# Router stage of an attention and mixture-of-experts kernel: older batches' work moved ahead of the new batch's in each step

## The reference, cut to what matters

```python
x = x + _layernorm(_L0_attn_ref(_layernorm(x), ...))          # x: 16 batches x 1024 tokens x 256
x = x + _layernorm(_L0_ffn_ref(_layernorm(x), ...))
# end of _L0_attn_ref:  attn = attn * rms * subln_g * (1 - LAMBDA_INIT);  return attn @ Wo
# start of _L0_ffn_ref, x here is the normalised one:
logits = jnp.einsum('bsd,ed->bse', x, gate_w) + gate_b        # 32 experts
probs = softmax(logits, axis=-2)                              # over the tokens
vals, idx = top 8 tokens of each expert and batch
merged = einsum('bked,bke->bed', x[idx], vals)                # weighted sum of the chosen tokens
# then two small expert layers on merged, and a scatter-add back to the tokens
```

## Time and profile before

| what | value |
|---|---|
| median of 3 runs | 5975.78 us (5975.41 to 5980.85) |
| the profiled execution | 5969.97 us, its span 5968.1 us |
| route, first projection to last copy | 5382.58 to 5699.74 us of the span |
| busy over the whole span | PE 94%, DVE 92%, ACT 83%, POOL 35% |

### The profile page before, as it was taken

The page is one execution under the profiler, slowest core; times in us unless marked ns, Lnnn a source line. Parts: engine busy times, 40 slices in busy tenths (PEclk is TensorE's granted clock), DMA queues, the critical chain, the costliest instruction groups (busy, mean ns, idle before and its releaser), DMA issues. The chain is left out here.

```text
span 5968.1 us, 167678 instructions
## 1 busy us (share of the span) xinstructions
PE 5593.6 (94%) x50896; PEld 1978.1 (33%) x50896; DVE 5489.2 (92%) x6110; ACT 4965.0 (83%) x9174; POOL 2070.4 (35%) x3560
## 2 busy tenths in 40 slices
PE   8878999999999999999999999999999999987776
PEld 4542333333333333333333333333333333325524
DVE  7868999999999999999999999999999999966716
ACT  6665999999999999999999999999999999983313
POOL 7981222222222222222222222222222222235506
PEclk9997999999999999999999999999999999998878
DMA  5671222232222222222232222222222222206587
GB/s 181 204 209 46 52 53 53 53 52 53 52 53 52 53 51 51 52 51 51 50 52 53 53 53 53 52 53 51 53 53 53 53 50 52 50 15 202 198 341 309
DMA packets 408166, 495.27 MB, mean 83 GB/s; under 512 B 132051, under 2 KB 265331, under 8 KB 395235
## 3 DMA queue, kind: packets, MB, share of 16 engines
q1 hardware_dynamic: 406499, 485.74, 32.5%
q10 hardware_dynamic: 1024, 0.53, 0.0%
HBM read 360.60 MB, written 123.21 MB: 81 GB/s over the span
## 5 line engine op out<-in xcount | busy, mean ns | idle before, releaser
L741 DVE TENSOR_REDUCE at_largest<-at_ps_m 128x1 f32<-128x1024 f32 x4096 | 4695.6, 1210 | 43.2 <-PE at_ps_m L845 28.7
L707 ACT ACTIVATE at_e<-at_ps_e 128x512 f32<-128x512 f32 x8192 | 4409.6, 598 | 351.8 <-PE at_ps_e L814 153.3
L831 PE MATMUL at_ps_o<-at_e,at_v 128*32 128x256 f32 (+1 forms) x30720 | 2680.3, 421 | 31.3 <-ACT at_e L707 20.6
L845 PE MATMUL at_ps_m<-k_stack,q_stack 48*128 48x512 bf16 x8192 | 2484.3, 384 | 87.8 <-DVE at_largest L741 55.6
L814 PE MATMUL at_ps_e<-q_stack,k_stack 51*128 51x512 bf16 x8192 | 2514.6, 382 | 8.4 <-issue 2.1
L831 PEld LDWEIGHTS at_ps_o<-at_e,at_v 128*32 128x32 f32 x30720 | 844.9, 149 | 1556.5 <-issue 818.0
L814 PEld LDWEIGHTS at_ps_e<-q_stack,k_stack 51*128 51x128 bf16 x8192 | 567.7, 93 | 1665.4 <-ACT at_e L707 1632.5
L626 POOL TENSOR_TENSOR at_negated<-at_zeros,at_largest_t 128x32 f32<-128x32 f32 x256 | 64.9, 254 | 2165.3 <-DVE at_largest_t L748 2165.3
L845 PEld LDWEIGHTS at_ps_m<-k_stack,q_stack 48*128 48x128 bf16 x8192 | 573.8, 93 | 219.8 <-DVE at_largest L741 188.2
L669 POOL TENSOR_TENSOR at_rms<-at_mean_eps,at_minus_half 128x16 f32<-128x16 f32 x128 | 372.8, 2912 | 10.0
L645 POOL TENSOR_TENSOR at_crossed<-at_totals 128x32 f32<-128x32 f32 x128 | 32.4, 253 | 750.8 <-DMA at_totals<-at_sums 750.8
(11 more groups left out here) (130 smaller groups left out, 3005.6 us busy)
## 6 DMA issues: line engine op xcount, KB each, us to landing
k_stack<-k_parts SPq DMA_DIRECT2D x1536, 64.0 KB
q_stack<-q_parts SPq DMA_DIRECT2D x256, 192.0 KB
q_stack<-q_parts SPq DMA_DIRECT2D x256, 128.0 KB
w_first<-in_w SPq DMA_DIRECT2D x32, 1024.0 KB, 23.4
ex_w_second<-in_w SPq DMA_DIRECT2D x32, 1024.0 KB, 26.1
q_parts<-pr_parts SPq DMA_DIRECT2D x96, 256.0 KB, 2.5
k_parts<-pr_parts SPq DMA_DIRECT2D x96, 256.0 KB, 2.8
pr_x_in<-in_x SPq DMA_DIRECT2D x16, 1024.0 KB, 5.7
```

Source lines behind the costliest of these rows:

```text
L707: nc.scalar.activation(e[:, j % E_BUFS], ps_e[:, bank(u, j)], ACT.Exp, scale=SCALE).then_inc(exp_done, 1)
L741: nc.vector.reduce_max(largest[:, u % 2, j // SIDE, j % SIDE:j % SIDE + 1], ps_m[:, j % 2], AX.X).then_inc(max_done, 1)
L831: last = nc.tensor.matmul(ps_o[32 * tile:32 * tile + 32, columns], v[:, u, tile // 2, first:first + 2 * VD * TILES - kt:TILES], e[:, (QUAD ...
L845: last = nc.tensor.matmul(ps_m[:, j % 2, half * HALF:(half + 1) * HALF], q_stack[rows, u, pair, c, t * P:(t + 1) * P], k_stack[rows, u, pa ...
```

## The change

In each step three engines take the older batches' work first. PE does two banks of transposes, the projection's first half, the other two banks, the projection's second half; then in odd steps the logits, and only after them the transposes of `picked`, which used to come before. ACT does its four copies before `norm_y(0)`, and the exponentials after `norm_y(0)` instead of last. DVE does both gate parts at the step's start. All instructions are the same ones in the same number; waits go with them.

```diff
 # ACT
-                    if y:
-                        act.wait_ge(x1_stored[u % 2], 16 * (2 * i + u // 2) + 16)
-                        norm_y(0)
                     if turn:
...
                             nc.scalar.copy(xn_t[:, u % 2, j % KC, (j // KC) * HALF:(j // KC + 1) * HALF],
                                            ps_t[:, bank(i, u, j)]).then_inc(t_copied, 1)
+                    if y:
+                        act.wait_ge(x1_stored[u % 2], 16 * (2 * i + u // 2) + 16)
+                        norm_y(0)
+                    if gate and u % 2 == 0:
+                        act.wait_ge(max_done, q + 1)
+                        nc.scalar.activation(weights[:], logits[:], ACT.Exp, ...)
                     if merge:
...
-                    if gate and u % 2 == 0:
-                        act.wait_ge(max_done, q + 1)
-                        nc.scalar.activation(weights[:], logits[:], ACT.Exp, ...)
 # DVE
-                    if y:
-                        y_statistics(0)
+                    if gate and u % 2 == 0:
+                        dve.wait_ge(logits_done, q + 1)
+                        nc.vector.tensor_scalar(logits[:], ps_l[0:ROWS], gate_b[:], None, ALU.add)...
+                        nc.vector.max(out=top[:], in_=logits[:])...
+                        nc.vector.tensor_scalar(neg_max[:], top[:, 0:1], -1.0, None, ALU.mult)...
                     if gate and u % 2 == 1:
...
+                    if y:
+                        y_statistics(0)
                     if norm:
...
                     if y:
                         y_statistics(1)
-                    if gate and u % 2 == 0:
...
 # PE
-                    if y:
-                        pe.wait_ge(attn_loaded[u % 2], 16 * (2 * i + u // 2 + 1))
-                        project(range(BANKS))
-                    if turn:
-                        pe.wait_ge(xn_done, n - 1)
-                        for j in range(TRANSPOSES):
+                    def transposes(banks):
+                        for j in banks:
...
+                    if turn:
+                        pe.wait_ge(xn_done, n - 1)
+                        transposes((0, 1))
+                    if y:
+                        pe.wait_ge(attn_loaded[u % 2], 16 * (2 * i + u // 2 + 1))
+                        project((0, 1))
+                    if turn:
+                        transposes((2, 3))
+                    if y:
+                        project((2, 3))
                     if turn and u % 2 == 1:
...
                         out.then_inc(logits_done, 1)
+                    if merge:
+                        pe.wait_ge(picked_done, q + 1)
...
```

More of the change, by code:

```diff
@@ L1103, in one @@
                                            ps_t[:, bank(i, u, j)]).then_inc(t_copied, 1)
+                    if y:
[3 more added lines that the diff above has]
+                        act.wait_ge(max_done, q + 1)
+                        nc.scalar.activation(weights[:], logits[:], ACT.Exp, bias=neg_max[:], accum_out=total[:]).then_inc(
+                            weights_done, 1)
                     if merge:
@@ L1115, in one @@
                                            "p (k b e) -> p k e b", k=KC, b=PAIR)).then_inc(t_copied, 1)
-                    if gate and u % 2 == 0:
-                        act.wait_ge(max_done, q + 1)
-                        nc.scalar.activation(weights[:], logits[:], ACT.Exp, bias=neg_max[:], accum_out=total[:]).then_inc(
-                            weights_done, 1)
                 rounds(act, one)
@@ L1148, in y_statistics @@
                         out.then_inc(y_var_done, 1)
-                    if y:
-                        y_statistics(0)
+                    if gate and u % 2 == 0:
+                        dve.wait_ge(logits_done, q + 1)
+                        nc.vector.tensor_scalar(logits[:], ps_l[0:ROWS], gate_b[:], None, ALU.add).then_inc(logits_read, 1)
+                        dve.wait_ge(logits_read, q + 1)
+                        dve.sem_inc(passed, 1)
+                        nc.vector.max(out=top[:], in_=logits[:]).then_inc(gate_step, 1)
+                        dve.wait_ge(gate_step, 4 * q + 1)
+                        nc.vector.tensor_scalar(neg_max[:], top[:, 0:1], -1.0, None, ALU.mult).then_inc(max_done, 1)
                     if gate and u % 2 == 1:
@@ L1246, in one @@
                         out.then_inc(logits_done, 1)
+                    if merge:
+                        pe.wait_ge(picked_done, q + 1)
+                        pe.wait_ge(t_copied, use + end + 1)
+                        pe.sem_inc(pe_passed, 1)
+                        for t in range(TILES):
+                            out = nc.tensor.transpose(ring[end][:, t * ROWS:(t + 1) * ROWS],
+                                                      picked[:, (u - 1) // 2, t * P:(t + 1) * P], ident[0:ROWS, 0:ROWS])
+                        out.then_inc(t_done, 1)
                     if merge:
```

## The result

The changed kernel takes 6004.88 us in the median (5999.81 to 6019.33, 5 runs) against 5977.04 of the kernel before: ratio 1.0047, 95% interval 1.0033 to 1.0061, or 28 us more. The forecast was 5992, with 6004.88 inside its range; it was slower, as forecast, by nearly twice the 16 us of the sum.

The account below looks back on a forecast made before the run. It took route to be bound by chains from engine to engine, no engine full. Start +7.4, steady part +6 and end +3 gave +16 us on the profiled 5969.97: 5986, and with the median 5.8 above, 5992, range 5974 to 6009.

Parts of the forecast that it names:

- What comes in their place: PE's transposes wait for xn, DVE's last write, with the projection queued behind: steps become one chain; pair 38.9 against 37.7 us.
- the last part of the prediction: What would show it right: PE waits for xn in every step, 7 us before odd ones, 2 to 3 before even.
- signs named: DVE's merge wait as long or longer, even xn tiles 4.7 us, odd step 22 to 23, even 16, route about 333.
- Odd step: From xn to xn, PE's chain with slow transposes after some 7 us idle: 22.6 us, bounds 22.0 to 23.5, before 20.3.
- two bounds, 0.46 and 1.9: Odd step's projection on PE: us lost to the lower clock, from logits and from projections behind slow transposes; 1.0 taken.
- Even step: From xn to xn: semaphore 0.13, transposes 1.0, projection to inverse root 10.43, xn 4.72; 16.3 us, bounds 14.3 to 17.7.
- The start: Steps 2 to 5: +8.4 for steps 2 and 3 with slow clock, -2.5 step 4, +1.5 step 5; together +7.4 us.
- The steady part: Last xn of step 5 to that of step 15: a pair 38.9 against 37.7 us, +6 over five pairs.
- The end: Step 16 +2.1 us, gate part ahead of statistics; step 17 +1, picked's transposes to merge no longer hidden; together +3.
- Rival A: PE and DVE lose their odd-step waits and nothing replaces them: 6.7 us a pair, 40 us gained, 5936; 10%.
- Rival B: Same chain but the clock stays up: 1.9 us less in each odd step and steps 2 and 3, 5977; 18%.
- Rival D: Same chain, worse: even steps' xn 6.14 us under POOL's sum, projection loses the full 1.9; +18, 6010; 12%.

Follow-up runs that it names:

- swap: Changed kernel with PE's projection halves each put ahead of a pair of transpose banks; 5971.71 us, ratio 0.9978 to the kernel before.
- filled: Changed kernel plus PE matmuls that nothing reads, 14 or 4, right before its wait for xn; 5989.41 us, ratio 1.0013 to the kernel before.
- act_alone: Kernel before with only ACT's order changed (four copies ahead of the normalisation's first half, exponentials after it); ratio 0.9976 to the kernel before.
- pe_as_before: Kernel before with ACT and DVE in the changed order, PE untouched; 5967.36 us, ratio 0.9972 to the kernel before.
- short_sum: Changed kernel with POOL's residual sum over 16 of 256 columns per tile; 5995.24 us, one run, against 5984.54 for the kernel before.

## Why the prediction was right, and where its size was off

The direction and the mechanism held: **What comes in their place**. PE's first work in a step waits for what DVE writes last, 7.2 us ahead of each odd step and 2.1 ahead of each even one, as the last part of the prediction said; the exchange in swap, which changes only that, removes the loss. Of the signs named, two missed: DVE's wait for the merge is a little shorter than before (31.8 against 33.6 us), and route is 347 us long, not 333.

By terms of the sum, route lost 30 us where 16 were forecast.

- **Odd step**, 22.6 forecast, 23.4 measured. At full clock it is 20.8 (filled); the forecast's terms without its 1.93 for the clock make 20.7. That the structure of the chain comes out right to 0.1 us is in part luck: in filled xn takes 3.2 us there, not 2.67, since it meets the end of POOL's sum, which the forecast did not count for the odd step's xn, and the other parts are together 0.4 shorter than their terms. In the changed kernel this xn takes 2.93. The clock's share was forecast as 0.93 for the transposes (right) and 1.0 for the projection; the projection's half lost 2.05 (5.67 - 3.62). I had two bounds, 0.46 and 1.9, and took the middle; in the steady part the upper one was it. (In steps 2 and 3, behind waits of 8.0 and 7.2 us, the half projection took 5.09 and 4.45, so the loss isn't a fixed price.)
- **Even step**, 16.3 forecast, 17.5 measured. This is the step of the working that failed: I let it run at full clock, since the wait ahead of it is short. The rows have 1.96 and 4.22, which is 0.9 and 0.6 more. At full clock it is 16.1 (filled). xn at 4.70 was right to 0.02, and POOL's inverse root ends 5543.58 - 5532.65 = 10.9 us after the projection's start, 10.43 plus the clock's part.
- **The start**, +7.4 forecast, +9.1 measured (from the first projection to the xn of step 5, 102.9 against 93.7 us). Steps 2 and 3, for which the slow clock was counted, took 18.4 and 17.7 against 18.2; steps 4 and 5, 17.7 and 23.2 against 16.3 and 22.6, the same two misses as in the steady part.
- **The steady part**, +6 forecast, +16 measured (204.6 against 188.6 us): the 2 us a pair of the first two points, five times.
- **The end**, +3 forecast, +4.8 measured (39.6 against 34.8). Step 16 took 10.9, against the 10.8 of the sum; from there on 2.7 were lost instead of 1. By the rows of the two traces, ACT's exponentials for the last pair stand behind the copies of merged, and the merge now comes after the transposes of picked and their copy; so from the reading of the last logits to the last transposes of picked it is 8.98 us (5716.00 to 5724.98) instead of 7.48 (5684.37 to 5691.85), 1.5 more. The last transposes of picked and the last merge, at a lower clock, take 1.07 and 6.15 us instead of 0.68 and 5.25, 1.3 more. No run tests these two.

Rival A, the gain, is a gain of the ACT part, not of the change: act_alone and pe_as_before have it, at 0.24 and 0.28% (14 and 17 us), at most some two fifths of the 40 that I gave it, since much of DVE's wait for the merge stays (21.3 of 33.6 us in act_alone's steady part). Rival B said that the chain would cost next to nothing if the clock stayed up, and filled comes near that, 1.0013 (1.0004 to 1.0022) where rival B's 5977 is 1.0002; its fault was mainly that the clock did not stay up by itself. Rival D named the right size for the projection's slow half but joined it to an xn of 6.14, which did not come. My 18% for B and 12% for D were two views of one question, how much clock the waits cost, and I answered it in the middle. For the even step's short wait the kernel before had one row on either side: in step 1 a wait of 1.99 us ended in a projection of 7.14 us, at full clock, and in step 2 one of 2.74 us in a projection of 8.70:

```profile
5393.34 7.14 PE L1211 MATMUL ro_ps_y<-ro_wo,ro_attn 128*128 128x256 f32 x32 [1.99 <-ACT ro_x L1090]
...
5403.22 8.70 PE L1211 MATMUL ro_ps_y<-ro_wo,ro_attn 128*128 128x256 f32 x32 [2.74 <-ACT ro_x L1090]
```

The forecast wait of 2 to 3 us lay between the two, so the rows didn't decide it; they should have made the slow clock in the even step a rival with a price and a chance, instead of nothing.

## What to carry to other kernels

In an in-order queue, put what depends on the previous step's last result behind work that is ready, even if that result is older: here exchanging the projection's halves with the pairs of transposes, on one engine, is worth 0.7% (swap against the changed kernel, 0.9978 to 1.0047). A move on one engine has to be priced with the orders of the others: the same gate part on DVE cost 0.17% or nothing, and the same order on PE 0.75% (0.9972 to 1.0047) or 2.6% (5980.26 to 6137.84 us, one run). When a change puts idle time in front of a TensorE burst, look for the clock that rows behind waits of like length show, for the short waits too; where the rows disagree, carry both prices, and settle it by filling the wait with matmuls that nothing reads.

## What the runs showed of the hardware beyond that

TensorE came back from a wait of 2.14 us at its lower clock (0.52 granted from 5530.8 to 5534.0 us), and the loss behind waits of 2.1 and 7.2 us was 1.5 and 3.0 us (sums of the two rows of each above their 1.04 and 3.62). A short wait can go either way: waits of 1.99 us (kernel before, step 1) and 1.80 (short_sum) left the work behind them at full clock, waits of 1.89 (short_sum) and 2.74 us (kernel before, step 2) did not. Matmuls into a part of PSUM that nobody reads kept it at 1.00 over 184.5 us and shortened route by 26 us, at no visible cost to another engine: DVE's, ACT's and POOL's busy times are within 1.1 us of the changed kernel's.
